# Adding a quarter of the expert output rows to token sums in DRAM instead of scattering them with one-hot matmuls

## The reference

```python
buf = jnp.zeros((E, CAP + 1, H), x.dtype).at[se, slot].set(x[tok])[:, :CAP]
h = jax.nn.silu(jnp.einsum('ech,ehf->ecf', buf, w_gate)) * jnp.einsum('ech,ehf->ecf', buf, w_up)
out = jnp.einsum('ecf,efh->ech', h, w_down)
gathered = out[se, jnp.minimum(pos, CAP - 1)] * valid.astype(x.dtype)[:, None]
return jax.ops.segment_sum(gathered * w, tok, num_segments=Tn)
```

## Time and profile before

| | |
|---|---|
| median of 3 runs | 448.79 us |
| the profiled execution | 451.19 us |
| its span, first to last instruction | 449.3 us |
| mean granted TensorE clock | 0.954 |
| PE busy | 398.7 us, 89% |
| DVE busy | 357.3 us, 80% |
| ACT busy | 217.9 us, 48% |
| POOL busy | 103.6 us, 23% |
| DMA through the hardware queue / the software queue | 27.7% / 3.6% of 16 engines |

### The profile page before, as it was taken

One profiled execution on the slowest core, in us unless ns is written; L12 is line 12 of the kernel. 1 busy time (PEld: TensorE's weight loads), 2 busy tenths in 40 slices (PEclk: granted clock), 3 DMA queues, 4 the chain that ended last, 5 costly groups with the idle time before them and its releaser, 6 DMA issues.

```text
span 449.3 us, 5076 instructions
## 1 busy us (share of the span) xinstructions
PE 398.7 (89%) x1660; PEld 216.2 (48%) x1664; DVE 357.3 (80%) x659; ACT 217.9 (48%) x406; POOL 103.6 (23%) x76
## 2 busy tenths in 40 slices
PE   0978999989995799798999999999999899998683
PEld 0423464677942366575777773444443344333231
DVE  4999979788779479599989979527977966549995
ACT  3864656573285358357675673521111141157680
POOL 1000004200000426032300000147684754440000
PEclk9999888989999599899999999999999999999798
DMA  7940000550059319865766530540000000000011
GB/s 263 400 176 1 2 0 0 200 211 0 1 195 318 82 49 266 268 205 148 226 199 203 218 117 1 198 177 1 0 1 0 1 0 0 1 0 0 1 48 47
DMA packets 12251, 47.45 MB, mean 106 GB/s; under 512 B 2897, under 2 KB 5434, under 8 KB 9794
## 3 DMA queue, kind: packets, MB, share of 16 engines
q1 hardware_dynamic: 11074, 43.20, 27.7%
q0 software_dynamic: 1152, 3.93, 3.6%
HBM read 44.76 MB, written 2.37 MB: 105 GB/s over the span
## 4 chain that ended last, share of the span: by engine, by line
PE 58%; DVE 31%; DMA 4%; issue 3%; ACT 2%; SPq 0%; POOLq 0%; DVEq 0%
PE bank L1581 8%; PE bank L1717 7%; PE bank L1704 6%; PE bank L1610 4%; PE bank L1636 4%; PE bank L1446 4%; PE bank L1749 3%; PE bank L1746 3%; DMA arena<-in_w_down 3%; PE bank L1672 2%; PE bank L1497 2%; PE bank L1356 2%; PE bank L1478 2%; PE bank L1562 1%; DVE ekT L1320 1%
## 5 line engine op out<-in xcount | busy, mean ns | idle before, releaser
L686 ACT ACTIVATE early<-bank 128x512 f32<-128x512 f32 (+1 forms) x24 | 14.3, 596 | 86.0 <-PE bank L1717 76.6
L1581 PE MATMUL bank<-onehot,rows 128*128 128x512 f32 x192 | 51.0, 405 | 0.0
L1245 DVE TENSOR_TENSOR early<-early,bank 128x512 f32<-128x512 f32 (+1 forms) x24 | 16.4, 685 | 37.8 <-ACT early L686 33.2
L1717 PE MATMUL bank<-arena 128*128 128x512 f32 (+1 forms) x96 | 42.2, 600 | 0.1
L1581 PEld LDWEIGHTS bank<-onehot,rows 128*128 128x128 f32 x192 | 33.9, 188 | 10.5 <-issue 4.1
L1704 PE MATMUL bank<-cT,arena 128*128 128x512 f32 x80 | 37.9, 596 | 0.0
L400 POOL TENSOR_TENSOR early<-early,arena 128x512 f32<-128x512 f32 (+1 forms) x12 | 20.0, 1669 | 74.5 <-DMA arena<-pair_weights 67.6
L389 POOL DMA_INDIRECT arena<-token_rows,arena x24 | 26.0, 1083 | 47.0 <-PE bank L1619 33.4
L406 POOL TENSOR_TENSOR early<-early,arena 128x512 f32<-128x512 f32 x10 | 22.3, 2230 | 29.3 <-DVE early L1245 29.3
L1717 PEld LDWEIGHTS bank<-arena 128*128 128x128 f32 (+1 forms) x96 | 15.7, 181 | 22.6 <-issue 21.2
L1610 PE MATMUL bank<-arena 128*64 128x192 f32 x256 | 24.2, 345 | 2.6 <-DMA arena<-in_w_down 2.5
(11 more groups left out here) (371 smaller groups left out, 862.5 us busy)
## 6 DMA issues: line engine op xcount, KB each, us to landing
arena<-in_w_gateup SPq DMA_DIRECT2D x16, 768.0 KB, 7.2
arena<-in_w_down SPq DMA_DIRECT2D x8, 768.0 KB, 10.2
arena<-in_wq SPq DMA_DIRECT2D x1, 2048.0 KB
arena<-in_wo SPq DMA_DIRECT2D x1, 2048.0 KB, 7.8
const<-in_const SPq DMA_DIRECT2D x1, 1688.0 KB, 10.9
arena<-in_w_upgate SPq DMA_DIRECT2D x1, 1408.0 KB, 5.8
kT<-in_kT SPq DMA_DIRECT2D x2, 512.0 KB, 5.8
xT<-in_xT SPq DMA_DIRECT2D x1, 1024.0 KB, 8.5
```

The source lines that it names most:

```text
L1581: return mm(bank[2 * ct + ch][:], rows1[:, i % RRING, part, ct * P:(ct + 1) * P], onehot1[:, t, ch * CHUNK:(ch + 1) * CHUNK], start=False, ...
L1717: last = mm(dst, (bup, bga)[z][:, f * P:f * P + fw], ((zu1, zg1), (zud, zgd))[k][z][:, ch * CHUNK:(ch + 1) * CHUNK], start=False, stop=Tru ...
```

## The change

Of the first six groups, tile 0 is no longer scattered by matmuls (ADDED; the other 18 tiles are PLACED). ACT writes it once, exact, and last of its group's three. GpSimd then issues one indirect DMA that adds its 128 rows to rows of a DRAM tensor, expert_sums. There are three sums (NACC), chosen by the slot's expert modulo 3, because one tile holds up to four experts' slots and a token may occur under several. In each sum, partition p has 16 rows (ACCROWS): rows 0 to 7 are its tokens, row 8 takes the empty slots. Each addition waits for the one before. At the start of the kernel GpSimd clears the sums by three DMAs from a tile of zeros. After the last addition SP loads the three sums side by side (1 MB each, into accs, ekT and ekvT), GpSimd adds them in two instructions of 128x2048, and PE brings the total into banks 0 to 3 by 16 products with the identity, 128 columns each, ahead of the last tile of each channel half. On DVE the remainders move behind the second piece of gate work, and five small operations compute the row numbers. Some semaphores are merged; const gets four columns.

```diff
+ADDED = [(g, t) for g in range(6) for t in (0,)]
+PLACED = [(g, t) for g in range(NG) for t in range(GT) if (g, t) not in ADDED]
+NACC, ACCROWS = 3, 16
...
+        def outbuf(g, t):
+            return outw2[:] if t == 0 and g % 2 else outw[:, t, :]
+        def out_order(g):
+            return (1, 2, 0) if (g, 0) in ADDED else (0, 1, 2)
+        def out_count(g, t):
+            return GT * g + out_order(g).index(t) + 1
...
             for g in range(2, NG):
                 experts(g)
+            sp.wait_ge(S("scaled"), 4 * CT + 2 * CT)
+            sp.wait_ge(S("acc_added"), 16 * (NACC + len(ADDED)))
+            for a, dst in enumerate((accs.rearrange("p t c -> p (t c)"), ekT[:].rearrange("p t c -> p (t c)"), ekvT[:].rearrange("p t c -> p (t c)"))):
+                sp.dma_start(dst, sums[a * P * ACCROWS:(a + 1) * P * ACCROWS, :].rearrange("(p r) c -> p (r c)", r=ACCROWS)[:, 0:NT * C]
+                             ).then_inc(S("acc_in"), 16)
...
+            step(g.memset(zeros, 0.0))
...
+            for a in range(NACC):
+                g.dma_start(sums[a * P * ACCROWS:(a + 1) * P * ACCROWS, :].rearrange("(p r) c -> p (r c)", r=ACCROWS)[:, 0:(NT + 1) * C],
+                            zeros).then_inc(S("acc_added"), 16)
+            pool.wait_ge(S("acc_added"), 16 * NACC)
...
+            def add_rows(g1, t):
+                n, i = ADDED.index((g1, t)), g1 * GT + t
+                pool.wait_ge(S("outw_ready"), out_count(g1, t))
+                pool.wait_ge(S("acc_added"), 16 * (NACC + n))
+                g.indirect_dma_start(sums[:, :], bass.IndirectOffsetOnAxis(ap=tokacc[:, i:i + 1].bitcast(U32), axis=0),
+                                     outbuf(g1, t), None, compute_op=ALU.add).then_inc(S("acc_added"), 16)
+            gathers(0)
+            gathers(1)
+            pool.wait_ge(S("h1_turned"), 2)
+            gathers(2)
+            gathers(3)
+            for g1 in range(6):
+                add_rows(g1, 0)
+                if g1 + 4 < NG:
+                    pool.wait_ge(S("h1_turned"), 2 * (g1 + 2))
+                    gathers(g1 + 4)
+            total = accs.rearrange("p t c -> p (t c)")
+            pool.wait_ge(S("acc_in"), 16 * NACC)
+            step(g.tensor_tensor(total, total, ekT[:].rearrange("p t c -> p (t c)"), ALU.add))
+            g.tensor_tensor(total, total, ekvT[:].rearrange("p t c -> p (t c)"), ALU.add).then_inc(S("sums_ready"), 1)
...
             shared_product(1)
+            rowbits, rest = tokacc.bitcast(U32), tokbits.bitcast(U32)
+            v.tensor_scalar(rowbits, tokf, float(N), spare, ALU.is_ge, ALU.mult)
...
                 for t in range(GT - 1):
-                    slot_onehot(g, t)
-                for t in range(GT):
-                    slot_rest(g, t)
-
+                    if (g, t) in PLACED:
+                        slot_onehot(g, t)
                 if g == 1:
                     forth(2, 1, 1)
...
                 if g == 6:
                     back_again(3, 1, 1)
+                for t in range(GT):
+                    if (g, t) in PLACED:
+                        slot_rest(g, t)
...
+            def sums_to_banks(ct):
+                pe.wait_ge(S("sums_ready"), 1)
+                for t in range(NT):
+                    mm(bank[2 * ct + t // 4][:, t % 4 * P:(t % 4 + 1) * P], accs[:, t, ct * P:(ct + 1) * P], ident,
+                       start=False, stop=False, skip_group_check=True)
...
             for ct in range(CT):
                 for t in range(GT):
+                    if t == GT - 1:
+                        sums_to_banks(ct)
                     last = scatter(NG - 1, t, ct)
```

More of the change, by code:

```diff
@@ L82 @@
 K_PL = K_EM + ST * E1
-K_W = K_PL + 2 * GE
+K_ACC = K_PL + 2 * GE
+K_W = K_ACC + GT + 1
 V_W, V_U, V_WR, V_LN1, V_LN2 = 0, 8, 16, 18, 20
@@ L206, in build @@
         ws1, wr1 = at(o, NT), at(o + 8, NT); o += 16
-        tokf, toki, wslot = at(o, ST), at(o + ST, ST), at(o + 2 * ST, ST); o += 3 * ST
+        tokf, toki, wslot, tokacc, tokbits = (at(o + ST * i, ST) for i in range(5)); o += 5 * ST
         assert o <= AC, o
@@ L638, in _ @@
                     scaled(3, 1)
-                for t in range(GT):
+                for t in out_order(g):
                     i = g * GT + t
@@ L1048, in _ @@
             shared_product(1)
+            rowbits, rest = tokacc.bitcast(U32), tokbits.bitcast(U32)
+            v.tensor_scalar(rowbits, tokf, float(N), spare, ALU.is_ge, ALU.mult)
+            dve.wait_ge(S("toki_ready"), 1)
+            step(v.tensor_scalar(rest, toki.bitcast(U32), P - 1, 4, ALU.bitwise_and, ALU.logical_shift_left))
+            step(v.scalar_tensor_tensor(rowbits, toki.bitcast(U32), 7, rowbits, ALU.logical_shift_right, ALU.bitwise_or))
+            step(v.tensor_tensor(rowbits, rowbits, rest, ALU.bitwise_or))
+            step(v.tensor_tensor(rowbits.rearrange("p (g t) -> p g t", t=GT), rowbits.rearrange("p (g t) -> p g t", t=GT),
+                                 accbits.unsqueeze(1).to_broadcast([P, NG, GT]), ALU.bitwise_or))
             dve.wait_ge(S("gather0"), 16 * GT)
@@ L1557, in _ @@
                           start=True, stop=True)
-            last.then_inc(S("slotT_done"), 1)
+            last.then_inc(S("counts1_done"), 1)
             def shared_down(ct, ch):
@@ L1576, in scatter_one @@
             def scatter_one(g, t, ct, part, ch):
-                i = g * GT + t
-                pe.wait_ge(S("onehot1_ready"), i + 1)
-                pe.wait_ge(S("rows1_ready"), i + 1)
-                return mm(bank[2 * ct + ch][:], rows1[:, i % RRING, part, ct * P:(ct + 1) * P],
-                          onehot1[:, t, ch * CHUNK:(ch + 1) * CHUNK], start=False, stop=(i == ST - 1 and part == 1))
+                n = PLACED.index((g, t))
+                pe.wait_ge(S("onehot1_ready"), n + 1)
+                pe.wait_ge(S("rows1_ready"), n + 1)
+                return mm(bank[2 * ct + ch][:], rows1[:, n % RRING, part, ct * P:(ct + 1) * P],
+                          onehot1[:, n % GT, ch * CHUNK:(ch + 1) * CHUNK], start=False, stop=((g, t) == PLACED[-1] and part == 1))
+            def sums_to_banks(ct):
[3 more added lines that the diff above has]
+                       start=False, stop=False, skip_group_check=True)
             def scatter_run(g, first, n):
-                for k in range(first, first + n):
-                    t, ct, part, ch = k // 8, k // 4 % 2, k // 2 % 2, k % 2
+                tiles = [t for t in range(GT) if (g, t) in PLACED]
+                for k in range(first, min(first + n, 8 * len(tiles))):
+                    t, ct, part, ch = tiles[k // 8], k // 4 % 2, k // 2 % 2, k % 2
                     last = scatter_one(g, t, ct, part, ch)
@@ L1896, in constants @@
     k[:, K_PL:K_PL + GE] = (p[:, None] % GE == np.arange(GE))
-    k[:, K_PL + GE:] = (p[:, None] % E1 // GE == np.arange(GE))
+    k[:, K_PL + GE:K_ACC] = (p[:, None] % E1 // GE == np.arange(GE))
+    expert = slot[0:GT].T // CAP
+    k[:, K_ACC + GT] = ACCROWS * p
+    k[:, K_ACC:K_ACC + GT] = (expert % NACC * P * ACCROWS).astype(np.uint32).view(np.float32)
     return k
```

79 lines of the change are left out of this document (43 added, 36 removed).

## The result

The changed kernel took 456.17 us (median of 4 runs, 454.53 to 457.29), the kernel before 447.70 (4 runs, 446.07 to 450.64): ratio 1.0146, 95% interval 1.0101 to 1.0192. (The ratios in this document are estimates with an interval. The plain quotient of these two medians is 1.0189, inside that interval; the four runs of the kernel before spread over 1%.) The change is slower, by about 1.5% where the forecast of 452.8 had 0.9%. The time is inside the stated range of 445.0 to 457.5, 1.3 us from its upper end. The profiled execution took 457.29 us (span 455.5), that of before 451.19 (span 449.3): 6.1 us apart.

What follows compares the result with a forecast made beforehand. PE bounds the kernel with DVE nearly as full; loop gain 5.9 less 0.8 us, but the end of the stage slips 3.6, up to 1.7 more for the clock: +4 on the median 448.79, so 452.8 us, range 445.0 to 457.5.

Steps and rivals of the forecast that it cites:

- rival 2: End of stage: last addition lands at 8.8 us, loads in at 253, adds hold up group 7; about 457, chance 0.14.
- D(7): Start of DVE's L1085 product of group 7, marking the loop's gain: forecast 248.3 with the first addition's cost, against 253.37.
- D(3) to D(6): Starts of DVE's L1085 product in groups 3 to 6: forecast 202.65, 213.65, 224.85 and about 234.8.
- The front: Start of the kernel: GpSimd's clearing of 3.5 MB in DRAM is covered, cost 0; without cover up to 9 us.
- My 0.8 us for the first addition: Loop: first addition, issued near 174 while DMA is full with weights PE awaits, costs 0.8 us; bounds 0 and 1.3.
- The first wait: PE's wait at iteration 2, for weights landing at 184.86 before the change, was to end at 185.7.
- the turns: End of stage: GpSimd's two 5.08 us additions and DVE's operations take turns by whole instruction, one turn 5.1 us.
- the landing of the last addition: Reading back: the last addition lands 4 us after issue, like a gather; loads issued at 237.4, all in at 248.2.
- my 23.2: End of stage as forecast, from group 7's L1085 product on DVE at 248.3 to layer 2's start at 271.5.
- the products: End of stage: eight new 128-column products on PE take 1.0 us per channel half, priced from transposes.
- Rival 1: End of stage: GpSimd's long adds leave DVE running and the sums are in time; 445.7 us, not slower, chance 0.25.
- Rival 3: Loop: DVE follows PE, moved remainders close more gaps, gain up to 9 us; 442.6 us, chance 0.06.

Runs made afterwards that it cites:

- without a read-back: Changed kernel whose three sums are never loaded, added by GpSimd or brought in by PE products; the additions in DRAM stay: 443.19 us, ratio 0.9878 to the kernel before.
- the run without additions: Kernel without loads, GpSimd sums and identity products, here also without the six DRAM additions and the clearing stores: 445.02 us, ratio 0.9895 to the kernel before.
- four groups: Changed kernel with tile 0 of only the first four groups added in DRAM instead of six; also called the four-group run: 455.65 us, ratio 1.0142.
- the eight-piece run: Changed kernel with GpSimd's two sums of 128x2048 cut into eight of 128x512: 455.63 us, ratio 1.0139.
- the run without GpSimd's sums: Changed kernel without GpSimd's two additions; the three loads and sixteen identity products stay, the products taking only the first sum: 449.60 us, ratio 0.9996.
- five groups: Changed kernel with five groups' first tiles added instead of six, and DVE making the sums in group 7 ahead of its remainders: 456.21 us, ratio 1.0161.

## Why the prediction was right, and where not

**What came is rival 2.** The forecast had the path right (a gain in the loop, GpSimd's sums shutting DVE out, PE idle and then at the low clock, slower in the end) and 4.0 us for the loss. By the ratio it is about 6.5. What the trace shows is rival 2 as it was written: the addition lands after 8.6 us (8.8 there), the loads are in at 252.9 (253), the one-hots and remainders of group 7 are held up, 456.17 (457). I had given it a chance of 0.14. The range holds the result because it was drawn as far as that rival.

**Right: the loop.** D(7) was set at 248.3 and came at 248.48, with D(3) to D(6) at 201.45, 212.79, 224.76 and 235.32, each within 1.2 us of its forecast. That this execution came within 0.2 at D(7) is luck, as the spread over nine kernels shows (241.64 to 248.91); the ratio without a read-back gives a gain of 5.5 us, between 3 and 8. The run with the reordering alone (1.0005) and the run without additions (0.9895 against 0.9878) carry two of its zeros: the reorder is free, and so are the transfers in the loop, as far as can be measured. The front cost nothing either: L1464, the L1399 of before, starts at 48.26 (48.48 before), and DVE still waits 4.24 us for the first gather. My 0.8 us for the first addition has nothing to show for it. The first wait ended near where I put it (185.39 against 185.7), but it was another wait: PE stood 5.02 us for a gather at 175.72, one issued at 165.81, and none for the weights. Other kernels of this study with the same additions (in eight pieces, and four groups) waited 3.3 to 3.9 us for the weights instead. That the number fits is partly luck.

**Right: the turns.** The forecast gave GpSimd two additions of 5.08 us; they took 4.98 and 4.83. It said that a DVE operation would be shut out for as long as one lasts; 0.42 became 4.72, and the eight-piece run shows the stretch shrinking with the instruction. By the Trainium skill ("GPSIMD Engine Reference", 3.1) each would take 4497 ns; the spans in the trace are 7 to 11% longer. Part of each span is GpSimd's own turn to wait: a one-hot of DVE was still running when each began, until 253.48 and 258.49, and from there on 4.45 and 4.35 us are left, 1 to 3% below the page's figure. The operation shut out first is a one-hot with a single SBUF matrix as input, 2.75 us here and 4.54 in the four-group run. I had quoted the Trainium skill ("SBUF — State Buffer", Who interferes with whom) for operations with two inputs; the same section says that copies, casts and tensor_scalar can hold the port pair too, in their two-port modes. The stretched one-hot, a tensor_scalar, fits that; no row shows in which mode it ran.

**Mis-sized: the landing of the last addition.** I took 4 us, that of a gather. It took 8.6, from its issue at 234.28. Its predecessor took 11.1, and GpSimd waited 9.94 us until that had landed, but little of this wait counts: ACT had the rows ready only at 232.57. By the 0.44 us from ACT's row to the issue in the run without GpSimd's sums, the addition would have gone out at about 233.0, 1.3 us sooner (an estimate); in the other eight kernels with six additions it waited for ACT. The loads went out at 242.94 instead of 237.4 and were in at 252.9 instead of 248.2. (In the forecast 3.1 MB at 400 GB/s should be 7.9 us, not 7.5; from first issue to the last landing the loads took 10.0 where it had 10.8.)

Lateness carries only part. Where the sums began at D(7), as I had assumed, the four-group run's end cost 22.98 against my 23.2 (271.5 - 248.3), and with the late start it cost 25.42. That the 22.98 fits is luck again: it holds 1.4 us more for the products than I gave and 1.7 us of low clock (eight matmuls in 3.61 us), which the 23.2 leave out, and PE's idle time is shorter, 2.69 us.

**Mis-sized: the products.** 1.0 us for eight, from the transposes; they took 1.7, as two instructions each. The Trainium skill ("FP8 and Floating Point Precision", TensorE Precision Notes) gives four passes through the array for true fp32. An estimate by it: 4 x 128 columns at the granted 2.4 GHz (PEclk 1.00 from 266.65 to 268.35) are 0.21 us, and the trace agrees (1.70 us for eight, 0.21 each). The end has two sets: 1.4 us more than I gave. With the waits taken out, the read-back still costs 3.6 us (17.96 - 14.32), three quarters of this execution's gain in the loop.

**The sum.** Gain in the loop 4.9; GpSimd's sum 7.5, shown by taking it away, of which 5.8 idle and 1.5 clock; products 3.6; with 0.2 that the end without a read-back saves, layer 2 comes 6.0 us later, where the forecast had 3.6 and up to 1.7 for the clock. **Rival 1** fell with the stretched operations. **Rival 3** fell too: the loop gained 4.9 us, not 9.

**Open:** why an addition lands 7.3 to 11.1 us after its issue was not tried by itself. The load on the DMA seems only a part of it: between the additions, three gathers issued from 190 to 195 us and three from 216 to 219 landed after 4.1 and 5.2 us in the median. Nor was a kernel tried in which GpSimd adds as early as in the changed one and only the products are moved to the end.

## What to carry to other kernels

Price a detour at the place where it comes back: the thinned scatter gave 1.2% in a loop with room, and the read-back fell into a stretch of 14.6 us in which PE had no gap and needed DVE's last rows. GpSimd is no spare engine beside a DVE that has work: count its additions as DVE's time, then ask whether DVE would do them in half of it (2.29 against 4.98 us). And in an in-order queue put the consumer of the latest data last: moving sixteen products behind the placements took 1.0104 to 1.0004.

## What the runs showed of the hardware that I had not expected

- An fp32 product with an identity is two instructions and 0.21 us for 128x128, a transpose of the same width one and 0.12.
- An adding indirect DMA of 128 rows lands 7.3 to 11.1 us after issue (7.8, 7.3, 8.6, 10.4, 11.1 and 8.6 for the six of the changed kernel), where a gather of as many rows had a median of 3.7 in the same trace; six of them change the loop by nothing measurable.
- Of three loads of 1 MB, the last lands 9.1 us after its issue when a group's weights were issued 10 us before, and 15.5 to 15.9 (four and five groups) when they are issued right behind such weights: started 9 to 11 us earlier, they were in 3 to 4 us earlier.
- An addition of 128x2048 on GpSimd took 4.35 to 4.45 us once DVE's running operation had ended, and DVE's next one then waited until it was done.
- An addition of 128x512 on GpSimd beside a busy DVE took 1.29 to 2.36 us, 1.63 in the mean of eight with the gaps between them (13.05 / 8), against 1.27 alone: cut in pieces, the sum is a third longer.
